# A routed block on one core: the last place's loads wait per block, four result buffers are added, and register loads are spread over the program

## The reference

```python
probs = softmax(xt @ w_router)                  # xt: 2048 tokens x 256, 16 experts
top_w, top_i = top_k(probs, 4)                  # 4 of 16 experts for each token
top_w = top_w / sum(top_w)
g = silu(einsum('td,edh->teh', xt, we1)) * einsum('td,edh->teh', xt, we3)
moe_out = einsum('teh,ehd->td', g * cw[:, :, None], we2)    # cw: top_w at top_i, else 0
shared = silu(xt @ ws1) * (xt @ ws3) @ ws2      # hidden width 512, done as 4 slices of 128
out = shared / 5 + moe_out * (4 / 5)
return x + gb * out
```

## Time and profile before

| what | value |
|---|---|
| runs | 345.56, 345.75, 346.32 us; median 345.75 |
| the profiled execution | 346.29 us, of which the span from the first to the last instruction is 344.2 us |
| granted TensorE clock | 0.998 of full speed |
| PE busy | 324.0 us, 94% of the span |
| DVE busy | 255.5 us, 74% |
| ACT busy | 196.4 us, 57% |
| POOL busy | 204.3 us, 59% |

### The profile page before, as it was taken

How to read it: one execution, slowest core, us unless ns; L and a number is a source line. 1 busy time by engine, 2 the same in 40 slices (tenths; PEclk the granted TensorE clock), 3 DMA queues, 4 the chain that set the end, 5 groups by cost and what they waited for, 6 DMA issues and landing times.

```text
span 344.2 us, 7783 instructions
## 1 busy us (share of the span) xinstructions
PE 324.0 (94%) x2298; PEld 299.7 (87%) x2298; DVE 255.5 (74%) x793; ACT 196.4 (57%) x439; POOL 204.3 (59%) x278
## 2 busy tenths in 40 slices
PE   6988999998889999999999988999999999999994
PEld 4787899998778999988878878999999999998883
DVE  1889999889978887466898756665656666669696
ACT  2467878775676855665443315666666666666210
POOL 1578855431787867467778401666666666667710
PEclk9999999999999999999999999999999999999999
DMA  6414920000112269773222165777776664989755
GB/s 214 154 50 171 288 94 18 15 17 17 70 69 91 100 193 349 234 236 121 103 103 105 70 170 141 236 230 228 228 223 195 195 208 152 292 316 389 239 194 169
DMA packets 43353, 57.55 MB, mean 167 GB/s; under 512 B 6225, under 2 KB 35665, under 8 KB 43313
## 3 DMA queue, kind: packets, MB, share of 16 engines
q1 hardware_dynamic: 35360, 35.42, 34.3%
q0 software_dynamic: 6864, 19.80, 15.1%
q10 hardware_dynamic: 1088, 1.84, 1.6%
HBM read 32.64 MB, written 24.40 MB: 166 GB/s over the span
## 4 chain that ended last, share of the span: by engine, by line
PE 59%; DVE 20%; issue 9%; DMA 4%; POOL 4%; ACT 3%; DVEq 0%; SPq 0%; POOLq 0%; ACTq 0%
PE ps L1697 14%; PE ps L1698 13%; PE ps L1699 13%; PE ps L1860 5%; PE ps L2061 5%; PE ps L2087 2%; POOL y_rows L733 2%; DVE bn L1116 2%; DMA cols<-in_L_c_dram 1%; DMA y_in<-y_rows 1%; DVE negmax L1516 1%; DVE y_in L1390 1%; PE ps L1965 1%; DVE y_in L1400 1%; DMA y_rows<-y_sb,aside 1%
## 5 line engine op out<-in xcount | busy, mean ns | idle before, releaser
L733 POOL DMA_INDIRECT y_rows<-y_sb,aside x79 | 79.9, 1012 | 54.5 <-ACT y_sb L1004 41.1
L698 POOL DMA_INDIRECT xg_rows<-hrow,slot_u x64 | 67.0, 1047 | 20.8 <-issue 17.8
L1697 PE MATMUL ps<-rpool 128*128 128x256 f32 (+3 forms) x164 | 51.9, 316 | 5.0 <-DVE rpool L1141 3.1
L1699 PE MATMUL ps<-rpool 128*128 128x256 f32 (+3 forms) x164 | 48.1, 293 | 0.0
L1698 PE MATMUL ps<-rpool 128*128 128x256 f32 (+3 forms) x164 | 48.0, 293 | 0.0
L1697 PE MATMUL ps<-w_hi_routed,xT_hi 128*128 x158 | 45.2, 286 | 1.9 <-DVE xT_lo L1633 1.8
L1699 PE MATMUL ps<-w_hi_routed,xT_lo 128*128 x158 | 44.7, 283 | 0.0
L1698 PE MATMUL ps<-w_lo_routed,xT_hi 128*128 x158 | 44.7, 283 | 0.0
L1697 PEld LDWEIGHTS ps<-rpool 128*128 128x128 f32 x164 | 31.2, 190 | 8.4 <-DVE rpool L1141 5.2
L995 ACT ACTIVATE r_silu<-ps 128x256 f32<-128x256 f32 x40 | 15.3, 383 | 36.7 <-PE ps L1699 35.7
L1697 PEld LDWEIGHTS ps<-w_hi_routed,xT_hi 128*128 128x128 f32 x158 | 30.2, 191 | 2.7 <-issue 2.6
(11 more groups left out here) (225 smaller groups left out, 928.6 us busy)
## 6 DMA issues: line engine op xcount, KB each, us to landing
xs<-xg_rows SPq DMA_DIRECT2D x68, 144.0 KB
y_in<-y_rows SPq DMA_DIRECT2D x16, 512.0 KB, 6.6
xg_rows<-empty SPq DMA_DIRECT2D x4, 576.0 KB, 3.3
x_in<-in_L_attn_x_dram SPq DMA_DIRECT2D x16, 128.0 KB, 2.3
w_raw_routed<-in_L_ffn_we_dram SPq DMA_DIRECT2D x8, 256.0 KB, 5.6
out_dram<-x SPq DMA_DIRECT2D x16, 128.0 KB, 1.8
xs_own<-xg_rows SPq DMA_DIRECT2D x11, 144.0 KB
wmod_sb<-in_L_wmod_dram ACTq DMA_DIRECT2D x3, 512.0 KB, 5.6
```

The lines of the kernel that those rows point to most:

```text
L698: nc.gpsimd.indirect_dma_start(out=xg, out_offset=bass.IndirectOffsetOnAxis(ap=slot_u[:, t, k:k + 1].bitcast(U32), axis=0), in_=hrow[:, t, ...
L733: nc.gpsimd.indirect_dma_start(out=yb, out_offset=bass.IndirectOffsetOnAxis(ap=dest[:, 2 * n + i:2 * n + i + 1].bitcast(U32), axis=0), in_ ...
L1697: nc.tensor.matmul(dst, w[0], x_[0], start=first, stop=False)
L1699: return nc.tensor.matmul(dst, w[1], x_[0], start=False, stop=last)
```

## The change

There are four parts.

1. **The fourth place by blocks.** `marks` gets three more ends (28 counts instead of 16): for blocks 0, 1 and 2 of the last place, the tile of expert 15 that holds the block's last token. PE sums the tokens of expert 15 through each block with one more matmul in `tile_places`, for which `carry` keeps all blocks' counts; DVE has six more instructions in `route_marks`. SP waits for a block's own counts before each of the last place's loads, and these go in the order 0, 1, 2, 3.
2. **Buffers.** The results of pairs 36 to 39 go to `y_own`, which lies where the ring `xs` was, so ACT does not wait for pairs 32 to 35 to land. POOL waits for that instead before it sends them, so that the counts keep their meaning.
3. **Register loads.** SP reads one count after each pair's loads (pairs 4 to 31); PE reads eight pairs' experts in each of units 9, 10 and 11.
4. **The last stores.** The two tiles of a half of block 3 go out in one transfer of 256 KB, instead of two of 128 KB.

```diff
+ENDS = TOPK + NG - 1
+def end_of_place(k, b):
+    if k < TOPK - 1 or GROUP_OF[b] == NG - 1:
+        return k
+    return TOPK + GROUP_OF[b]
...
+        y_own = at("y_own", HR, [P, RING, 2, D])
...
+        def y_of(n):
+            if n < NPAIR - RING:
+                return y_sb[:, n % RING]
+            return y_own[:, n - (NPAIR - RING)]
...
-            sp.wait_ge(s_marks, 1)
-            counts = [[sp.value_load(marks[0:1, k, r:r + 1], min_val=32, max_val=16 * loads_of(NPAIR - RING + r))
-                       for r in range(RING)] for k in range(TOPK)]
+            def fetch_count(m):
+                k, r = divmod(m, RING)
+                if m == 0:
+                    sp.wait_ge(s_marks, 1)
+                counts[k, r] = sp.value_load(marks[0:1, k, r:r + 1], min_val=32,
+                                             max_val=16 * loads_of(NPAIR - RING + r))
...
                 load_rows(n, place[2 * (n % 8):2 * (n % 8) + 2], s_xs[n % RING])
+                if 0 <= n - RING < RING * ENDS:
+                    fetch_count(n - RING)
...
             for k in range(TOPK):
-                for r in range(RING):
-                    sp.wait_ge(s_back[r], counts[k][r])
-                for b in (3, 0, 1, 2):
+                for b in (3, 0, 1, 2) if k < TOPK - 1 else range(NB):
+                    if b == 3 or k == TOPK - 1:
+                        for r in range(RING):
+                            sp.wait_ge(s_back[r], counts[end_of_place(k, b), r])
...
-                for t in range((2 * NB - 2 + i) * BT // 2, (2 * NB - 1 + i) * BT // 2):
-                    sp.dma_start(out_t[t], x1[:, t, :]).then_inc(s_out, 16)
+                two = slice((2 * NB - 2 + i) * BT // 2, (2 * NB - 1 + i) * BT // 2)
+                sp.dma_start(out_t[two].rearrange("t p d -> p t d"), x1[:, two, :]).then_inc(s_out, 16)
...
                 pool.wait_ge(s_ry, n + 1)
+                if n >= NPAIR - RING:
+                    pool.wait_ge(s_back[r], 16 * loads_of(n - RING))
...
                 act.wait_ge(s_rdown, n + 1)
-                if n >= RING:
+                if RING <= n < NPAIR - RING:
                     act.wait_ge(s_back[r], 16 * loads_of(n - RING))
-                nc.scalar.activation(y_sb[:, r].rearrange("p i d -> p (i d)"), ps[:, 4 + n % 2, :], ACT.Copy
+                nc.scalar.activation(y_of(n).rearrange("p i d -> p (i d)"), ps[:, 4 + n % 2, :], ACT.Copy
...
+                nc.tensor.matmul(ps[:, Y1, COUNT_AT + E:COUNT_AT + E + NG - 1], ones[:],
+                                 carry[:, 1:NG, E - 1:E].rearrange("p g e -> p (g e)"), start=True, stop=True)
...
+                if n == UNITS_FIRST - HELD // 8:
+                    pe.wait_ge(s_places, 3)
+                if n >= UNITS_FIRST - HELD // 8:
+                    first = 8 * (n - UNITS_FIRST) + HELD
+                    load_experts(first, first + 8, first)
...
-            pe.wait_ge(s_places, 3)
-            for first in range(0, HELD, 8):
-                load_experts(first, first + 8, first)
             down(UNITS_FIRST - 1, range(0, BT // 2))
```

More of the change, by code:

```diff
@@ L1303, in route_marks @@
             def route_marks():
-                last = tb[:, 2, E - TOPK:E].rearrange("p (k n) -> p k n", n=1)
-                dve.wait_ge(s_mark_const, 1 + RING)
-                begun = over[:].rearrange("p a b -> p (a b)")[:, 0:TOPK * NPAIR]
-                link(nc.vector.tensor_tensor(begun.rearrange("p (k n) -> p k n", k=TOPK),
-                                             last.broadcast_to((P, TOPK, NPAIR)),
-                                             first_of[:].broadcast_to((P, TOPK, NPAIR)), ALU.is_gt))
@@ L1312, in route_marks @@
-                settle()
-                link(nc.vector.tensor_reduce(passed[:], begun.rearrange("p (k r n) -> p k r n", k=TOPK, r=RING), AX.X,
-                                             ALU.add))
-                settle()
-                nc.vector.scalar_tensor_tensor(out=marks[:], in0=passed[:], scalar=32.0, in1=sent_all[:],
+                so_far = ps[:, Y1, COUNT_AT + E:COUNT_AT + E + NG - 1].rearrange("p (g m) -> p g m", m=1)
+                begun_of = over[:, 0:NG - 1, :]
+                link(nc.vector.tensor_tensor(begun_of, so_far.broadcast_to((P, NG - 1, E)),
+                                             steps[:].rearrange("p (g m) -> p g m", g=1).broadcast_to((P, NG - 1, E)),
+                                             ALU.is_gt))
@@ new lines, in route_marks @@
+                for first, end in ((0, TOPK), (TOPK, ENDS)):
+                    n = end - first
+                    begun = over[:].rearrange("p a b -> p (a b)")[:, 0:n * NPAIR]
+                    link(nc.vector.tensor_tensor(begun.rearrange("p (k n) -> p k n", k=n),
+                                                 last_tile[:, first:end, :].broadcast_to((P, n, NPAIR)),
+                                                 first_of[:].broadcast_to((P, n, NPAIR)), ALU.is_gt))
+                    settle()
+                    link(nc.vector.tensor_reduce(passed[:, first:end, :],
+                                                 begun.rearrange("p (k r n) -> p k r n", k=n, r=RING), AX.X, ALU.add))
+                    settle()
@@ L1317, in route_marks @@
+                nc.vector.scalar_tensor_tensor(out=marks[:], in0=passed[:], scalar=32.0,
+                                               in1=sent_all[:].broadcast_to((P, ENDS, RING)),
                                                op0=ALU.mult, op1=ALU.min).then_inc(s_marks, 1)
@@ L1818, in tile_places @@
                 pe.wait_ge(s_carry, NG)
-                nc.tensor.matmul(ps[:, Y1, COUNT_AT:COUNT_AT + E], ones[:], carry[:, NG % 2, :], start=True, stop=True)
+                nc.tensor.matmul(ps[:, Y1, COUNT_AT:COUNT_AT + E], ones[:], carry[:, NG, :], start=True, stop=True)
+                nc.tensor.matmul(ps[:, Y1, COUNT_AT + E:COUNT_AT + E + NG - 1], ones[:],
+                                 carry[:, 1:NG, E - 1:E].rearrange("p g e -> p (g e)"), start=True, stop=True)
             def tile_values():
@@ L2013, in last_logits, with load_experts @@
                        ).then_inc(s_lg_mm, 1)
+            HELD = 24
+            expert = [nc.alloc_register(PE_ENGINE, f"expert{n}") for n in range(2 * HELD)]
+            def load_experts(first, end, to):
+                pe.load(expert[2 * to:2 * (to + end - first)], places[0:1, 2 * NTL + 2 * first:2 * NTL + 2 * end])
             transpose_back(TILES - 2)
@@ L2037, in _ @@
             gate_up(UNITS_FIRST)
-            HELD = 24
-            expert = [nc.alloc_register(PE_ENGINE, f"expert{n}") for n in range(2 * HELD)]
-            def load_experts(first, end, to):
-                pe.load(expert[2 * to:2 * (to + end - first)], places[0:1, 2 * NTL + 2 * first:2 * NTL + 2 * end])
             def experts_of(n):
```

28 lines of the change are left out of this document (19 added, 9 removed).

## The result

The changed kernel takes **344.66 us** (median of 14 runs, 343.65 to 345.36). The kernel before, run beside it, took 346.5 us (14 runs, 344.99 to 348.83). The ratio is 0.9949, with a 95% interval of 0.9933 to 0.9966: 1.8 us less, between 1.2 and 2.3. The forecast was 344.6 us, from 1.12 us less. The profiled execution took 345.06 us with a span of 343.3, against 346.29 and 344.2.

What follows compares the result with a forecast made beforehand. Two chains, PE's and DVE's, 0.4 us apart, were taken to end the kernel, with the stores behind. 0.50 - 0.13 + 0.50 + 0.25 = 1.12 us off 345.75 gave 344.6 us, range 343.7 to 345.8.

Steps and rivals of the forecast that it cites:

- Register loads of PE: Units 9 to 11: loads hidden behind matmuls cost nothing; the pairs start 0.50 us earlier (bounds 0 and 0.77).
- More work ahead of the pairs: Before the pairs: extra count matmul costs 0.13 us (0 to 0.25); longer route_marks hides, taken as 0 (bounds 0 and 0.3).
- SP's counts: In the pairs: 28 reads of some 0.5 us each hide in SP's waiting, so loads of rows stay as early.
- The pairs: Loop of pairs: no term for its own length; only its start was put 0.50 us earlier.
- The tail: Place 3 to DVE's end: earlier block loads remove DVE's 0.94 us wait, buffers give PE 0.14; gain 0.50 us (0.1 to 0.94).
- the rival in which the counts do not come earlier: Tail: blocks 0 to 2 still wait for the last pair, DVE's 0.94 us stays; 345.0 us, chance 0.05.
- The last store: End of the kernel: one 256 KB transfer lands in 2.23 us; gain 0.25 us (bounds: gain 0.7, loss 0.8).
- The 2.6 us by the fit: Last store: the skill's estimate for 256 KB, by which it would lose 0.1 us instead of gaining 0.25; not adopted.
- Crowding: Tail: three early 512 KB loads beside sends of pairs 33 to 35 delay block 3's load; 346 or more, chance 0.05.
- the 0.9 that was to be seen: Trace sign at the tail's end: DVE's last instruction some 0.9 us earlier.

Runs made afterwards that it cites:

- v2: Changed kernel without the blocks' counts (order 0, 1, 2, 3 kept), PE's loads in the pairs halved, DVE's first register load ahead of g_step(12): 343.13 us, ratio 0.99.
- e9: Changed kernel with all 28 counts read ahead of the first load of rows, none in the pairs: 354.76 us in one run.
- e10: Changed kernel in which SP reads every count twice, 56 reads instead of 28: 348.35 us in one run.
- e7: Changed kernel in which PE reads four pairs' experts at a time within the pairs instead of eight: 343.9 us against 346.42 for the kernel before, ratio 0.9909.
- e6: Changed kernel in which each block of place 3 waits for the whole place, order 0, 1, 2, 3: 344.84 us against 346.42 for the kernel before, ratio 0.9946.
- e8: Kernel before with place 3's loads issued in the order 0, 1, 2, 3 instead of 3, 0, 1, 2: 346.06 us against 345.58, ratio 1.0015.
- e4: Changed kernel with the last four tiles of 128 KB stored one by one again: 344.91 us, ratio 0.9964.
- e5: Changed kernel without the four result buffers, so ACT waits again for pairs 32 to 35: 347.25 us against 346.42 for the kernel before, ratio 1.0016.
- e1: Kernel before with only PE's three register loads moved to units 9 to 11: 345.55 us against 346.21, ratio 0.9978.
- v3: v2 with DVE also reading eight registers at a time instead of sixteen: 342.94 us against 345.58 for the kernel before, ratio 0.991.

## Why the prediction was right, and where its steps were not

**Register loads of PE**: right. `xT_lo` of pair 0 started at 203.03, 0.50 us earlier by the stage in the table, and DVE's own load is what held it; moving that in v2 gave the next 0.51.

**More work ahead of the pairs**: under-sized. From `carry` to `down(8)` it cost 0.32 us (mean of eight profiles with it, 112.25, less that of six without, 111.93), where the step said 0.13 and nothing for `route_marks`. PE's timeline of the changed kernel has the extra count:

```profile
159.37 0.36 PE L1867 MATMUL ps<-carry,ones 128*128 128x3 f32 x2
159.60 0.41 PE L1855 MATMUL ps<-chosen,earlier 128*128 128x64 f32 x2
```

It is 0.23 us to the next, though it makes 3 columns: like the first count of 16 columns it is two instructions, and that one took 0.14. Some 0.06 more is at `down(8)`, which follows the product ahead of it by 0.28 to 0.32 us in the eight profiles and by 0.23 in the six, for `gated` at 188.83, 0.39 us later than in the earlier trace rows and 0.57 later counted from `carry`. The step put that later start at 0.4 us and still took the lower bound.

**SP's counts** at nothing: right for 28 reads (e9), but e10 shows that the margin was less than as many again. A read cost more than the 0.5 us of the step: in the earlier trace rows 16 of them start over 10.0 us, 0.67 us each.

**The pairs**, which the forecast left as they were, are the step that failed by most. Their surplus was 0.9 to 1.1 us in the four profiles of the kernel before and its parts, and 1.1 to 1.5 in the six of the changed kernel's kind (without e10), a loss of about 0.4 by the means. All of it stands in the intervals with a register load: at PE's two loads the mean is 0.53 us in the four and 0.67 in the six, at DVE's four 0.47 and 0.72. So most of the loss is at DVE's loads, and e7, in which PE's cost nothing, takes away more than the change had added there. Why these loads cost more in the changed kernel is open, since SP's reads of counts are not the cause. The row of such loads, 1.1 to 1.3 us, stood in the earlier trace rows, and only those that moved were costed.

**The tail**: the sizes right, one reason wrong. DVE's 0.94 us went, and DVE then met PE's end as the step said: 0.37 us of catching up (forecast 0.50 - 0.14 = 0.36). But the reason given, that the blocks' counts let the loads start earlier, was not needed: in the changed kernel block 0 is both early and first of the four, and being first is enough. The step read `the order 0, 1, 2, 3` only as a detail, though such loads land one after the other, so that block 0, put first, comes 1.6 us sooner (324.73 is when the first landed before, and 326.30 block 0); e6 and e8 show that this alone suffices. For the same reason the rival in which the counts do not come earlier had its price wrong: e6 is that case, and DVE's 0.94 us went in it. PE's share, 0.14 us, came out at 0.04 to 0.60 in the four profiles without buffers (20.51 to 21.07, less 20.47).

**The last store**: 0.32 us in the two profiles, forecast 0.25, and 2.2 us to land as the line between the rows said. Half of the gain is the size and half SP's free queue (e4, e8), both of which the step had. The 2.6 us by the fit in the Trainium skill, DMA: Bandwidth & Descriptors, section Anatomy of one DMA, was too long here; that section fits transfers that GpSimd issues, and SP issues these.

**Crowding** did happen: pair 35 landed 2.2 us later. It cost nothing only because the buffers had taken ACT out of its way (e5). The rival's "DVE and ACT don't feel it" was wrong for ACT without them.

The two profiles add up: up to `carry` -0.19 (not the change), to `down(8)` +0.16, to pair 0 -0.49, pairs +0.52, PE's tail -0.24, DVE's -0.37, store -0.32: -0.93 us, the difference of the spans. DVE's last instruction ended 0.61 us earlier (341.19 to 340.58), not the 0.9 that was to be seen. So 344.6 was met in part by luck, with one loss unforeseen and one gain that these profiles don't hold: the forecast took 1.12 us from 345.75, the runs differ by 1.8 us, from 346.5, and by 1.45 in the medians of their spans (342.9, and 344.35 for the kernel before beside e1 to e4). That the ring cost the kernel before more in other executions than in the profiled one would fit: its spans there reach from 342.8 to 347.5 us, those of the changed kernel from 341.9 to 343.6. But no profile of a long execution of the kernel before was taken, and this stays open.

## What to carry to other kernels

When a group of transfers is waited for as a whole, look first at which of them is issued first: putting the one that is wanted first in front was worth as much in the trace as counts of their own (a matmul and six instructions of DVE more), by which three of them start 8 to 9 us earlier, land only 1.2 to 1.7 us earlier (the changed kernel beside e6) and disturb the sends besides. A load of registers in a loop that is bound by one engine has to be shorter than that engine's queued work; split it rather than move it. And a ring's waits have to be priced together with whatever a change puts beside its transfers: without the early loads the wait that the buffers take away cost PE 0.04 to 0.60 us, beside them 2.3 us.

## What was not expected of the hardware

From pair 4 on a pair takes 2.807 us to within 0.01 us, except where a register load stands or rows come late. In the pairs a load of 16 registers took 1.10 to 1.39 us on PE, one of 8 took 0.59 to 0.78, and up to 0.2 us more to the next instruction. In units 9 to 11 the length of a load goes with its place: the first took 1.44 to 1.55 us, the second 1.11 to 1.13, and the third 1.31 to 1.34 in the eight kernels with the blocks' counts and 1.11 in the three without (e1, v2, v3). So the spread is not chance alone; what it hangs on is shown by no run here. Four loads of 512 KB that were issued together landed one after the other in the order of issue, 1.6 to 1.9 us apart (325.36, 326.95, 328.56 and 330.44 in e6).
